# A transformer block on eight cores: three attention weights loaded over SP and cast by engines, FFN weight loads split between SP's and POOL's queues

## What is computed

```python
x = x + attn(layernorm(x), Wq, bq, Wk, bk, Wv, bv, Wo, bo)
x = x + ffn(layernorm(x), w1, s1, w2, s2, h1, sh1, h2, sh2, w3, s3)
# attn: q, k, v = x@W + b; softmax(q k^T / 8) v in each window of 128 rows
#       (start every 64), window outputs added, divided by their count; @Wo + bo
#       (all 1024 columns in one score: the windows are not split into heads)
# ffn:
h = silu(x @ w1.T * s1) * (x @ w2.T * s2)      # 1024 -> 4096
h = gelu(h @ h1.T * sh1)                       # 4096 -> 4096
h = gelu(h @ h2.T * sh2)                       # 4096 -> 4096
y = h @ w3.T * s3                              # 4096 -> 1024
```

## Time and profile before

| | us |
|---|---|
| median of 3 runs (lowest to highest) | 7010.14 (6675.91 to 7507.52) |
| the profiled execution | 6682.15 |
| its span, slowest core (6) | 6680.5 |
| spans of the 8 cores | 6664.4 to 6680.5 |
| TensorE matmul busy | 5734.2 (86%) |
| VectorE, ScalarE, POOL busy | 952.7, 647.8, 167.9 |

### The profile page before, as it was taken

The page is one execution under the profiler, slowest core; times in us unless marked ns, Lnnn a source line. Parts: engine busy times, 40 slices in busy tenths (PEclk is TensorE's granted clock), DMA queues, the critical chain, the costliest instruction groups (busy, mean ns, idle before and its releaser), DMA issues.

```text
span 6680.5 us, 74712 instructions; the slowest of 8 cores (6664.4 to 6680.5 us)
## 1 busy us (share of the span) xinstructions
PE 5734.2 (86%) x27888; PEld 2756.3 (41%) x28409; DVE 952.7 (14%) x2375; ACT 647.8 (10%) x1085; POOL 167.9 (3%) x205
## 2 busy tenths in 40 slices
PE   2155558879998999799989997999799989998998
PEld 1033335534443444344434443444344434443444
DVE  1133336630002000200020002000200020002000
ACT  0000000011001100110011001100110010001010
POOL 0000001100000000000000000000000000000000
PEclk8577779989999999999999999999999999999999
DMA  9999981134443444344434443444344434433443
GB/s 139 114 123 124 125 113 42 36 108 152 154 155 130 150 154 153 126 152 154 152 128 151 153 154 125 155 151 158 132 146 154 148 134 155 153 139 133 151 151 139
DMA packets 143157, 913.05 MB, mean 137 GB/s; under 512 B 16016, under 2 KB 16080, under 8 KB 65760
## 3 DMA queue, kind: packets, MB, share of 16 engines
q1 hardware_dynamic: 119808, 738.25, 31.4%
q0 software_dynamic: 23008, 169.99, 16.5%
HBM read 974.76 MB, written 126.35 MB: 165 GB/s over the span
## 4 chain that ended last, share of the span: by engine, by line
PE 78%; another core or an unknown queue 7%; DMA 7%; DVE 4%; issue 3%; ACT 1%; DVEq 0%; POOL 0%; ACTq 0%; SPq 0%; POOLq 0%
PE Z L860 52%; PE Z L899 6%; PE Z L799 5%; PE Z L813 5%; DMA p_w12r<-w12s 5%; PE Z L577 3%; PE Z L640 2%; PE Z L612 2%; PE Z L530 1%; DMA p_bq<-bq 1%; PE Z L768 0%; PE Z L422 0%; DVE f_lnfm L772 0%; DVE a_lnfm L406 0%
## 5 line engine op out<-in xcount | busy, mean ns | idle before, releaser
L860 PE MATMUL Z<-f_aT,p_wbig 128*128 128x512 bf16 x8032 | 1761.3, 379 | 9.4 <-DMA p_wbig<-h1s 0.6
L860 PE MATMUL Z<-f_bT,p_wbig 128*128 128x512 bf16 x8024 | 1760.7, 379 | 9.1 <-DMA p_wbig<-h2s 0.3
L860 PEld LDWEIGHTS Z<-f_aT,p_wbig 128*128 128x128 bf16 x8192 | 801.4, 98 | 968.0 <-issue 2.9
L860 PEld LDWEIGHTS Z<-f_bT,p_wbig 128*128 128x128 bf16 x8192 | 801.4, 98 | 967.1 <-issue 1.3
L914 DVE TENSOR_SCALAR f_o3T<-Z,p_s 128x512 f32<-128x512 f32 x64 | 48.0, 750 | 3932.5 <-PE Z L899 3932.5
L577 PE MATMUL Z<-a_lnfm,a_wq 128*128 128x256 bf16 (+1 forms) x1088 | 148.8, 306 | 505.3 <-DVE a_wot L538 502.5
L799 PE MATMUL Z<-f_lnfm,p_w12r 128*128 128x512 bf16 x1992 | 484.5, 382 | 103.0 <-DMA p_w12r<-w12s 93.1
L813 PE MATMUL Z<-f_lnfm,p_w12r 128*128 128x512 bf16 x2016 | 483.9, 381 | 11.1 <-DVE f_ost L932 9.4
L899 PE MATMUL Z<-f_aT,p_wbig 128*128 128x512 bf16 x2008 | 441.5, 379 | 2.5 <-DMA p_wbig<-w3s 0.3
L799 PEld LDWEIGHTS Z<-f_lnfm,p_w12r 128*128 128x128 bf16 x2048 | 189.0, 98 | 380.5 <-issue 187.2
L577 PEld LDWEIGHTS Z<-a_lnfm,a_wq 128*128 128x128 bf16 x1088 | 116.6, 111 | 538.4 <-issue 509.4
(11 more groups left out here) (81 smaller groups left out, 1933.7 us busy)
## 6 DMA issues: line engine op xcount, KB each, us to landing
p_wbig<-h1s SPq DMA_DIRECT2D x256, 1024.0 KB, 4.8
p_wbig<-h2s SPq DMA_DIRECT2D x256, 1024.0 KB, 4.8
p_w12r<-w12s SPq DMA_DIRECT2D x256, 512.0 KB, 3.4
p_wbig<-w3s SPq DMA_DIRECT2D x64, 1024.0 KB, 4.8
h1s<-h1b POOLq DMA_DIRECT2D x8, 4096.0 KB, 200.1
h2s<-h2b POOLq DMA_DIRECT2D x8, 4096.0 KB, 116.5
a_x<-x_ext POOLq DMA_DIRECT2D x33, 512.0 KB, 51.5
xms<-a_xm POOLq DMA_DIRECT2D x33, 512.0 KB, 3.6
```

The source lines that it names most:

```text
L860: N0=N0: e.matmul(zb[:, 0:N0], wbig[ws][:, ic * 128:ic * 128 + 128], src[:, ic * TPMAX:ic * TPMAX + N0], start=(ic == 0), stop=(ic == NHC ...
```

## The change

**Start.** The bias bq and its scaling come first. Only wq is still cast by a POOL DMA. wk, wv and wo are read in float32, in halves of 2 MB, by SP into one staging buffer `a_stg`; halves are turned into bf16 by VectorE and ScalarE in turn (L302 and L306 of the new file). Each load waits for the conversion before it. `a_stg` lies over the buffers `xmst` and `wotmp`, so the first `wo_tile`s wait for the last conversion. The order of emission puts these conversions ahead of the first `ln_stats`.

**FFN.** Blocks with an even number are loaded by SP and those with an odd number by POOL, in all four stages. For passes 1 to 7, the first two w12 blocks are issued by POOL at the head of `ffn_stage_a` (L761 of the new file).

```diff
-    cast_w("wq", wq_s)
-    cast_w("wk", wk_s)
-    cast_w("wv", wv_s)
     sm = E("gp", lambda e: e.dma_start(out=bq8[:], in_=bq_in), ...
     bq8ev = E("dv", lambda e: e.tensor_scalar_mul(bq8[:], bq8[:], 0.125), ...
+    cast_w("wq", wq_s)
     load_x(2)
     load_x(3)
-    cast_w("wo", wo_s)
+    stg = ar.al("a_stg", [128, 4096], F32, at=ar.offset_of(xmst[0]))
+    prev_conv = None
+    cvi = 0
+    for nm, dst in (("wk", wk_s), ("wv", wv_s), ("wo", wo_s)):
+        evs = []
+        for h in range(2):
+            ld = E("sy", lambda e, s=w_in[nm], h=h: e.dma_start(
+                out=stg[:], in_=s[:, h * 4096:(h + 1) * 4096]),
+                waits=[prev_conv], inc=sd, inc_by=16)
+            if cvi % 2 == 0:
+                cv = E("dv", lambda e, d=dst, h=h: e.tensor_copy(
+                    d[:, h * 4096:(h + 1) * 4096], stg[:]),
+                    waits=[ld], inc=dv)
+            else:
+                cv = E("ac", lambda e, d=dst, h=h: e.copy(
+                    d[:, h * 4096:(h + 1) * 4096], stg[:]),
+                    waits=[ld], inc=ac)
+            cvi += 1
+            prev_conv = cv
+            evs.append(cv)
+        wcast[nm] = tuple(evs)
+    stg_done = prev_conv
...
     def ffn_stage_a(p):
         tiles = FFN_PASSES[p]
+        if p >= 1:
+            for sl in (0, 1):
+                w12_pref[(p, sl)] = E("gp", lambda e, sl=sl: e.dma_start(
+                    out=w12r[sl][:], in_=w12s[sl]),
+                    waits=[conv_ev[("w12", 0)], w12_free[sl]],
+                    inc=gd, inc_by=16)
...
-            d1 = E("sy", lambda e, oc=oc, sl=sl1: e.dma_start(
-                out=w12r[sl][:], in_=w12s[oc]),
-                waits=[conv_ev[("w12", oc // 8)], w12_free[sl1]],
-                inc=sd, inc_by=16)
+            d1 = w12_pref.pop((p, oc), None)
+            if d1 is None:
+                eng, pool = ("sy", sd) if oc % 2 == 0 else ("gp", gd)
+                d1 = E(eng, lambda e, oc=oc, sl=sl1: e.dma_start(
+                    out=w12r[sl][:], in_=w12s[oc]),
+                    waits=[conv_ev[("w12", oc // 8)], w12_free[sl1]],
+                    inc=pool, inc_by=16)
...
-                dd = E("sy", lambda e, pc=pc, hs=hsrc, ws=wslot: e.dma_start(
+                eng, pool = ("sy", sd) if pc % 2 == 0 else ("gp", gd)
+                dd = E(eng, lambda e, pc=pc, hs=hsrc, ws=wslot: e.dma_start(
...
-            dd = E("sy", lambda e, oc=oc, ws=wslot: e.dma_start(
+            eng, pool = ("sy", sd) if oc % 2 == 0 else ("gp", gd)
+            dd = E(eng, lambda e, oc=oc, ws=wslot: e.dma_start(
```

More of the change, by code:

```diff
@@ L541, in wo_tile @@
                 waits=[mmlast, ld_ev["bob"],
-                       wotmp_free[u % 2] if oh == 0 else None], inc=dv)
+                       wotmp_free[u % 2] if oh == 0 else None,
+                       stg_done if (u <= 1 and oh == 0) else None], inc=dv)
             bank_free[pi] = ev
@@ L547, in wo_tile @@
             waits=[ev, xle[u],
-                   xmid_spill[u - 2] if u >= 2 else None], inc=po)
+                   xmid_spill[u - 2] if u >= 2 else None,
+                   stg_done if u <= 1 else None], inc=po)
         wotmp_free[u % 2] = pl
@@ L725, in build_nc @@
     f_en_ring = [None, None]
+    w12_pref = {}
     def emit_reload(t):
```

## The result

The changed kernel is slower by 1.3%: the ratio to the kernel before, in runs on one chip, is 1.0134 with a 95% interval of 1.0118 to 1.015. That is 89 us on the 6660 to 6690 us of this kernel. It takes 6770 to 6780 us, where the kernel before takes 6676 to 6690; the forecast was 6849. The direction was right, and the size, 167 us or 2.5%, nearly twice what was measured.

What follows compares the result with a forecast made beforehand. Bounds: DMA at the start and until 990 us, then attention's engines; in w12 the two-slot ring, in h1 and h2 TensorE. Sum: 6682 + 0 + 128 + 10 - 6 + 35 = 6849 us, range 6670 to 7080.

Steps and rivals of the forecast that it cites:

- the pair: Two successive w12 blocks, one per slot: 7.7 us measured before the change, 8.7 forecast, 6.91 without waits.
- The start, 0: Up to x tile 4: 41 us of float32 loads against 39 us saved on POOL's queue, late group 0 covered; net 0.
- the cover of 34 us: At the start: time group 1 has to spare before x tile 6 arrives, taken to hide the late group 0.
- Rival (c): Start: 16 KB weight rows cut into 8 KB packets, 92 us per half with conversion; +110 us, 6959 us; chance 0.12.
- The w12 stage, +128: w12 loads of odd blocks: POOL's later issue and 4.3 us landing add 1.0 us to each of 128 pairs.
- Rival (b): w12: POOL landing 3.7 us, pair 8.1, costing 51 us; 1 MB loads fit; 6737 us; chance 0.12.
- The early issue, nothing: Head of FFN passes: issuing w12 blocks 0 and 1 early from POOL gains nothing, as SP already issued them early.
- -6: First w12 blocks: two of four reloads move to the end of w3, saving about 1 us in each of six passes.
- The last blocks, +10: End of w12: SP's first h1 load shares the engines with POOL's block 31, about 1.3 us per pass, +10 us.
- h1, h2 and w3, +35: 288 loads of 1 MB on POOL landing in 5.9 us only just fit; 0.12 us each, +35 us.
- (a): FFN loads: POOL's are no slower once its queue is in use, pairs stay at 7.7; 6686 us; chance 0.20.
- (d): w12 and start: two queues leave no load late, pairs fall to 6.91, start gains 39 us; 6542 us; chance 0.06.

## Why the prediction was off, point by point

**What bounds the kernel.** This held. The two-slot ring is what makes w12 wait: a third slot takes the pair to 6.91 us, the prediction's "free of waits" figure. Attention was bound by the conversions until 990.

**The start, 0.** Right, and by its steps: halves of 51 to 53 us (48), the last conversion at 259 (243), statistics at 206 ("about 200"), the first Q matmul at 272 (250), x tile 6 at 389 as before. The start alone measured 1.0005. Of the cover of 34 us some 5 were used, since VectorE's wait ends at the same time and is 4.7 us shorter. Rival (c), with 92 us for a half, fell: the packets of these loads are of 16 KB, 128 to a half.

**The w12 stage, +128.** The failed step is here: the term for the landing of a POOL load was mis-sized, and with it the pair. Of the 78 us by which the forecast overshot, the w12 stage holds 71 (132 against 61). The prediction took 4.3 us from the first of the reloads, a 0.9 us handicap against SP; it is 3.6, a handicap of 0.3. That is under the 3.7 us that the prediction itself had named as a sign that it is wrong. The rest of the formula held: 3.45 + 0.65 + 3.6 + 0.3 = 8.0, the pair read above, where 8.7 was forecast.

Two smaller slips stand beside it. The 8.7 was built from single durations and set against a measured mean of 7.7, though the same formula gives only 7.1 for SP; the spread of the landings was in one and not in the other. It turned out small, 8.20 in the mean against 8.0. And the pair price was applied to 128 pairs, though it had been measured on the 96 in the middle, and the ends of the stage had terms of their own. 96 x (8.20 - 7.64) = 54, -8 for the first four blocks and +16 for the last four make 62, and 61 were measured.

Rival (b) had the mechanism with the right landing, 3.7 and 8.1 us a pair. Its total, 6737, was 35 us under 6772 (1.0134 times the profiled execution). It had 55 us for the w12 stages with their ends, where 61 were measured, and nothing for the large loads, where 16 were; that its 55 came so near is partly luck, since its pair rose by 0.4 over 128 pairs and the measured one by 0.56 over 96. The Trainium skill, "DMA: Bandwidth & Descriptors", "Latency and other measured facts", on which (b) leaned (1 us against 0.6 to the first byte), comes near to the measured 0.3 us. The other half of the cost is the hop from the releasing engine to the issue, 0.60 us on POOL and 0.13 on SP.

Why was the first reload slower than a steady load? It was one of several issued 0.5 to 0.6 us apart, and they share the 16 engines. I took its extra time for a property of POOL's queue. The w12 blocks 0 and 1 show that it isn't one. In the kernel before SP issues them 0.5 us apart behind a 1 MB load; in the changed kernel POOL does so, 0.6 us apart; with h1, h2 and w3 by SP, POOL issues them 6 to 10 us apart. Their landings on core 1, in this order (the first is that of pass 1 alone):

```profile
DMA to landing us min/median/max: 5.6/6.0/6.3
```
```profile
DMA to landing us min/median/max: 3.7/6.4/8.9
```
```profile
DMA to landing us min/median/max: 3.4/4.0/5.1
```

In a burst SP's loads are nearly as slow as POOL's, and spread out POOL's are nearly as fast as in steady use. What part of the 4.3 us of a first reload is due to the loads behind it wasn't tried.

**The early issue, nothing.** As a comparison with the kernel before this is right: the first four blocks take 8 us less, where -6 was forecast. That the two agree is luck in part: the -6 was forecast for another cause, reloads moved away. As a statement on the part it was wrong. Without it the split costs 60 us more, since POOL's weight load would stand behind the stores. The prediction looked at where SP had issued these loads and never asked where POOL would, had they not been moved ahead.

**The last blocks, +10.** 16 us measured; the mechanism (h1's loads beside POOL's block 31) showed itself when both h1 loads were on SP, with 28 us and more and a later landing of block 31.

**h1, h2 and w3, +35.** 16 us measured in these stages of the changed kernel, and some 30 (24 in h1 and h2, 6 in w3) where they alone were split. The prediction's reasoning had an error. The landing is 5.1 to 5.3, not 5.9, so a load has 0.7 us to spare in the median, and only the tail is late. SP's loads may take 6.91 - 0.13 - 0.3 = 6.48 us, and in the kernel before 12 to 20 of its 576 on cores 0 to 3 took longer. POOL's later issue lowers that limit to 5.96 us, and 10 to 62 of its 288 take longer in the changed kernel, 71 to 89 where the large loads alone were split. The factor of two in the cost goes with these counts and not with the medians, which are alike. Why the tail differs between the two kernels isn't settled.

**The other rivals.** (a), no cost, fell by the 8.20 us pairs. (d), faster, fell too: a slot on POOL would have had to land in 2.4 us, and the minimum is 3.4.

## What to carry to other kernels

A load that is issued when its slot comes free has a period of work + hop from the releasing engine to the issue + landing + pickup; the slowest slot sets it, so a move onto a slower queue can only lose there, while one more slot removed the whole term here. Take the landing from a load that runs alone and not from the first of a burst, and when a load moves to an engine with other work, look at what stands ahead of it there at every border. A stage with its DMA engines at 0.98 beside one where they are at 0.14 was worth more than all of this: spreading the transfers gave 3.8% with one line.

## What the runs showed of the hardware that was not expected

- A load issued by POOL lands only 0.2 to 0.3 us later than SP's in steady use (3.6 against 3.3 us for 512 KB, 5.1 against 4.9 for 1 MB, core 1).
- That landing isn't the same on all cores: in the run with three slots and the split, core 2's median for 1 MB by POOL was 6.1 us, core 1's 5.1, with SP's at 4.8 on both. On core 2 the rows list 35 waits for these loads in h1 and h2, on core 1 nine. Counted from the starts of the matmuls, 146 of the 256 odd blocks start late on core 2 and 30 on core 1, 44 and 14 us in all. The cause is open.

```profile
  PE Z L897: 10.0, 35
...
DMA to landing us min/median/max: 4.9/6.1/8.5
```

- A 2 MB load over SP's queue took 51 to 53 us beside conversions on POOL's queue. The prediction had this from the earlier trace rows. From 95 to 206 us SP's queue had 288 packets and 4.19 MB, POOL's 353 packets and 10.52 MB, and while a half was under way the packets of both queues alternated evenly, those of SP of 16 KB and those of POOL of 32 KB. The queue with the larger packets so got five times the engines' time.

```profile
q0 software_dynamic: 353, 10.52, 83.4%
q1 hardware_dynamic: 288, 4.19, 16.0%
```

- After a pause of 10.75 us TensorE's next 8 matmuls took 3.57 us at a granted clock of 0.50 and the 8 after them 2.96, where 1.89 is usual. A late load of this length so costs some 2.7 us more than its wait.
